# Local attention: masks and turned keys ahead of the output product, statistics at the unit's end

## What is computed

```python
h = shift_token(x)                     # half the features from the row before
q, k, v = split(h @ wqkv)              # 8 heads of 64
q, k = l2norm(q) * qs, l2norm(k) * ks  # norm clipped from below at 1e-12
q, k = rotary_xpos(q, k)
# windows of 128 queries look at the window before and their own:
sim = where(mask, -max, (8 * q) @ k.T)
x = x + (softmax(sim) @ v) @ wo
```

## Time and profile before

| | us |
|---|---|
| median of 3 runs | 3652.75 |
| lowest, highest | 3647.45, 3654.94 |
| profiled execution, its own time | 3663.63 |
| its span, first to last instruction | 3661.8 |
| TensorE busy | 3324.7 (91%) |
| VectorE busy | 1947.9 (53%) |
| ScalarE busy | 1564.8 (43%) |
| GpSimd busy | 569.0 (16%) |
| mean granted TensorE clock | 0.955 |

### The profile page before, as it was taken

How to read it: one execution, slowest core, us unless ns; L and a number is a source line. 1 busy time by engine, 2 the same in 40 slices (tenths; PEclk the granted TensorE clock), 3 DMA queues, 4 the chain that set the end, 5 groups by cost and what they waited for, 6 DMA issues and landing times. The chain is left out here.

```text
span 3661.8 us, 47378 instructions
## 1 busy us (share of the span) xinstructions
PE 3324.7 (91%) x16112; PEld 1955.4 (53%) x16113; DVE 1947.9 (53%) x4733; ACT 1564.8 (43%) x3481; POOL 569.0 (16%) x591
## 2 busy tenths in 40 slices
PE   5999997786999969999998899998899899997998
PEld 3455555553666644444443566665555566665454
DVE  1999996341111125555553677776331677775332
ACT  1766662221222225554554566565221555554211
POOL 0000001442000058000000322221000211111112
PEclk8999998887999979999999999999999999998999
DMA  3000003103111121000000100000000100000000
GB/s 129 1 1 1 1 1 132 36 26 104 44 44 46 44 61 56 4 1 1 1 1 2 62 8 10 9 8 8 21 1 1 37 10 8 10 8 4 12 12 23
DMA packets 72644, 90.25 MB, mean 25 GB/s; under 512 B 10974, under 2 KB 61426, under 8 KB 72178
## 3 DMA queue, kind: packets, MB, share of 16 engines
q1 hardware_dynamic: 65186, 69.28, 5.7%
q0 software_dynamic: 7248, 18.26, 1.6%
HBM read 59.63 MB, written 24.12 MB: 23 GB/s over the span
## 5 line engine op out<-in xcount | busy, mean ns | idle before, releaser
L1619 DVE CUSTOM_DVE_ANT_0 sb_win_masked<-ps_win_pss,sb_win_around 128x384 f32<-128x384 f32 (+1 forms) x512 | 255.6, 538 | 229.9 <-PE ps_win_pss L1726 229.5
L2027 ACT ACTIVATE sb_loc_pr<-ps_loc_psw,sb_loc_nb,sb_loc_sc 128x256 f32<-128x256 f32 x512 | 281.0, 568 | 187.3 <-DVE sb_loc_nb L2154 187.3
L2230 PE MATMUL ps_loc_psa<-sb_stk_w,sb_loc_hT 128*128 128x512 f32 x768 | 350.1, 606 | 5.0 <-DMA sb_stk_wo<-in_loc_wo 3.3
L2517 PE MATMUL ps_mlp_ps<-sb_mlp_hT,sb_stk_w 128*128 128x512 f32 (+1 forms) x768 | 322.6, 613 | 22.3 <-DVE sb_mlp_hid L2470 22.3
L1544 ACT ACTIVATE sb_win_pT<-ps_win_pst 128x512 f32<-128x512 f32 x368 | 199.8, 595 | 207.0 <-PE ps_win_pst L1737 205.2
L2230 PEld LDWEIGHTS ps_loc_psa<-sb_stk_w,sb_loc_hT 128*128 128x128 f32 x768 | 142.0, 192 | 181.4 <-issue 177.8
L2517 PEld LDWEIGHTS ps_mlp_ps<-sb_mlp_hT,sb_stk_w 128*128 128x128 f32 (+1 forms) x768 | 130.2, 184 | 201.6 <-issue 201.6
L719 PE MATMUL ps_rec_psp<-sb_rec_hT,sb_rec_w 128*128 128x512 f32 x512 | 235.4, 603 | 1.0 <-ACT sb_rec_hT L422 1.0
L2470 DVE SCALAR_TENSOR_TENSOR sb_mlp_hid<-ps_mlp_ps,sb_stk_col,sb_mlp_gl 128x512 f32<-128x512 f32 x96 | 71.7, 749 | 303.3 <-ACT sb_mlp_gl L2439 303.3
L2439 ACT ACTIVATE sb_mlp_gl<-ps_mlp_ps,sb_stk_col 128x512 f32<-128x512 f32 x96 | 65.9, 687 | 381.8 <-PE ps_mlp_ps L2517 381.5
L1726 PE MATMUL ps_win_pss<-sb_win_kT,sb_win_q 32*128 32x384 f32 (+1 forms) x1024 | 224.0, 520 | 4.7 <-DVE sb_win_top L1619 3.0
(11 more groups left out here) (316 smaller groups left out, 6560.0 us busy)
## 6 DMA issues: line engine op xcount, KB each, us to landing
sb_exp_rows<-sorted_tokens SPq DMA_DIRECT2D x72, 128.0 KB, 2.0
expert_results<-sb_exp_res SPq DMA_DIRECT2D x72, 128.0 KB, 1.7
sb_keep_x<-in_x SPq DMA_DIRECT2D x1, 4096.0 KB, 23.1
sb_moe_w_in<-in_L_ffn_w_in_eDF SPq DMA_DIRECT2D x8, 512.0 KB, 11.3
sb_moe_w_sw<-in_L_ffn_w_swiglu_eDF SPq DMA_DIRECT2D x8, 512.0 KB, 11.5
sb_exp_w_out<-in_L_ffn_w_out_eFD SPq DMA_DIRECT2D x8, 512.0 KB, 7.0
sb_stk_angles<-in_angles SPq DMA_DIRECT2D x32, 128.0 KB, 3.7
out_y<-sb_stk_y SPq DMA_DIRECT2D x8, 512.0 KB, 3.0
```

Source lines behind the costliest of these rows:

```text
L1619: i = nc.vector.tensor_tensor_reduce(masked[:, pair % 2, j, 0:keys], pss[:, (n + j) % PLAIN, 0:keys], around[:, first:first + keys], 1.0, ...
L2027: e = nc.scalar.activation(pr[:, hf, h], psw[:, hf, h // 2, h % 2 * 256:h % 2 * 256 + 256], ACT.Exp, scale=sc8[:, b, hh:hh + 1], bias=nb[: ...
L2230: t = nc.tensor.matmul(psa[:, c], hT[:, b, k, 1 - k:P + 1 - k], w[:, k, c * 512:(c + 1) * 512], start=(k == 0), stop=(k == KD - 1))
L2517: i = nc.tensor.matmul(ps[at:at + M, q % 2, i2], w1[:, k, i2 * HID + f * P:i2 * HID + f * P + M], hT[:, b, k], start=(k == 0), stop=(k == ...
```

## The change

Five edits, all in `local_attention`. On TensorE, masks(i+1) and turn_keys(i+1) are issued between turn_queries(i+1) and output(i); masks(0) stands ahead of the loop. On VectorE, copy_keys(i+1) moves ahead of add_output(i), and statistics(i+4) to the end of the unit. On ScalarE, copy_input(i+2) goes ahead of deviation(i+4). The lower bound of the squared norms becomes a scalar_tensor_tensor with the same tile as both inputs, max(max(ss, 1e-24), ss), which gives the same value.

```diff
@@ scalar
+                    if i + 2 < TILES:
+                        copy_input(i + 2)
                     if L == 0 and i + 4 < TILES:
                         deviation(i + 4)
-                    if i + 2 < TILES:
-                        copy_input(i + 2)
@@ vector
-                    nc.vector.tensor_scalar(ss[:, b], ss[:, b], 1e-24, None, ALU.max).then_inc(s_ssm, 1)
+                    nc.vector.scalar_tensor_tensor(out=ss[:, b], in0=ss[:, b], scalar=1e-24, in1=ss[:, b], op0=ALU.max,
+                                                   op1=ALU.max).then_inc(s_ssm, 1)
@@
-                    if L == 0 and i + 4 < TILES:
-                        statistics(i + 4)
                     scale_output(i)
                     if i + 1 < TILES:
                         scale_keys(i + 1)
+                        copy_keys(i + 1)
                     add_output(i)
-                    if i + 1 < TILES:
-                        copy_keys(i + 1)
+                    if L == 0 and i + 4 < TILES:
+                        statistics(i + 4)
@@ tensor
+                masks(0)
                 for i in range(TILES):
-                    masks(i)
                     scores(i)
@@
                     if i + 1 < TILES:
                         turn_queries(i + 1)
+                        masks(i + 1)
+                        turn_keys(i + 1)
                     output(i)
-                    if i + 1 < TILES:
-                        turn_keys(i + 1)
```

## The result

The changed kernel takes 3625.61 us (median of 4 runs, 3624.12 to 3626.12), against 3653.85 us for the kernel before in the same comparison (4 runs, 3647.45 to 3658.14). That is 28.2 us less, a ratio of 0.9923 with a 95% interval of 0.9906 to 0.9941 (by these bounds 21.6 to 34.3 us). The forecast was 3627.5.

What follows compares the result with a forecast made beforehand. TensorE bounds the kernel, so only its waiting can be won: 28 units at 0.62 us (17.4) plus 34 at 0.23 (7.8) make 25.2 us off the 3652.75 median, 3627.5 us; range 3617 to 3641.

Steps and rivals of the forecast that it cites:

- Statistics, 0.39 us in 28 units: VectorE, pass 0: statistics moved to the unit's end let the output product start 0.39 us earlier in 28 units.
- unit 28: Pass 0 unit with the 0.70 us bound but no statistics; its output scaling starts 2.08 us after the value products start.
- The norm bound, nothing: VectorE's norm bound as scalar_tensor_tensor: taken as zero gain, even if it still takes 0.70 us.
- Masks and keys ahead: TensorE, before the output product: hides masks in the wait; scores 0.23 us earlier in pass 1, 0.62 with statistics moved.
- V+3.43: Turned keys' forecast start on TensorE, 3.43 us after V, the start of the value products (L2301).
- the step to the scores' shape: TensorE, from transposes to the scores' 64-row shape: price taken as 0.13 us, bounds zero and 0.26.
- V+6.04: Next scores' forecast start on TensorE, 6.04 us after the value products start, against 6.27 before in pass 1.
- (a): GpSimd's second product (L1916) holds up VectorE's L2136 in pass 0: 0.11 us in 28 units, 3630.6 us; chance 9%.
- (b): TensorE's reordering yields nothing, steps between masks, transposes and scores costing 0.23 us a unit more: 3641.8 us; chance 5%.
- (c): Statistics end last before VectorE's maxima, giving back 0.44 us in 28 units: 3639.8 us; chance 3%.
- (d): Denser TensorE work lowers the granted clock in both passes: 0.96 would give 3667 us, slower; chance 3%.

Runs made afterwards that it cites:

- the kernel with early reciprocal and other bank: Changed kernel plus input turned ahead, sums' reciprocal before rotated-key addition, turned sums written to the bank ScalarE empties: 3586.64 us against 3632.87 before, ratio 0.987.

## Why the prediction was right

**What bounds.** TensorE's waiting was all there was to win, and that is what went: TensorE's busy time by the page changed by 3 us, and the clock in the two stretches stayed at 1.00.

**Statistics, 0.39 us in 28 units.** Measured alone: units from 16.31 to 15.92. The reading of unit 28, which has the long bound but no statistics, was enough. What the prediction put less exactly is that the 0.41 us "are the statistics'": they belong to bound and statistics together, since a short bound brought units to 15.92 us as well.

**The norm bound, nothing.** Measured alone 0.9998. The rule from the Trainium skill (SBUF — State Buffer, Who interferes with whom) said that the new form, with its two SBUF inputs, would be held up too. The trace agrees: 0.70 us beside GpSimd's product, 0.19 us for the reduction, which the same section names as never contending. Two inputs are not the whole of it, since the old form with one was held for the same 0.70 us.

**Masks and keys ahead.** The chain on VectorE gave the keys' start at V+3.43 to the hundredth. The term that was mis-sized comes behind it. I took 1.83 us for the output product and 0.13 for the step to the scores' shape, and so V+6.04; the rows of after have 0.49 for the keys, 1.73 for the output product and 0.32 from the turned input to the scores, V+5.97. The 1.83 us were read from a unit in which the output product itself had waited. In the kernel with the masks alone ahead it does not wait, and there it takes 1.73 us to the start of the keys, and the keys 0.43. Now it is the keys that have waited (0.49), and the sum of the two is 2.22 instead of 2.26. The step of shape costs some 0.10 (0.32 less 0.22). Both together are 0.07 us in 62 units, 4 us: by units the change is worth 30 us (15.62 us a unit, where about 15.70 were forecast), and the forecast was 25.2. The measured 28.2 us, with its interval of 21.6 to 34.3, cannot tell the two apart. That the forecast time came within 2 us is thus partly luck.

**The range.** By its own terms, 8 us for the step and 4 for the median, it would be 3615.5 to 3639.5, not 3617 to 3641. The result lies in both.

**Rivals.** (a) L2137 begins beside L1916 and takes 0.68 us, no hold-up; it is GpSimd that is held when it starts second (L1924, 0.93 us instead of 0.46). (b) The reordering did not come out dearer: the steps cost less than taken, not more. (c) The maxima had 0.32 us to spare, 0.36 were worked out. (d) The clock stayed at 1.00 in both stretches.

## What to carry to other kernels

When an in-order engine waits for a short chain on another, list the work that is ready at that moment, put it there, and then follow each result it produces to its reader's queue: the masks and turned keys gained 0.31 us a unit with the keys' copy moved along, and lost 0.75 us (15.92 to 16.67, pass 1) with the copy left behind. A unit of the same loop that lacks one step is a free experiment; it priced the statistics and the bound before anything was built. And where two releasers end within 0.1 us of each other, the one that the trace names may be the wrong one, and only removing both shows their worth.

## What the runs showed of the hardware

A small VectorE instruction can take four times its own time beside GpSimd. The bound, 16 elements wide, takes 0.18 us with GpSimd idle and 0.70 us beside its product in two forms, of which one reads a single SBUF tile; as a reduction it takes 0.19 us at the same place. Where it began 0.16 us behind the start of the product instead of 0.06 (the kernel with early reciprocal and other bank), it took 0.59 us and again ended 0.03 us after the product. It works the other way as well: GpSimd's spread sums took 1.37 us instead of 1.04 when they began 0.16 us after VectorE's addition of two SBUF tiles, and its table 0.93 instead of 0.46 us when it began 0.07 us after VectorE's scaled keys. L2137 was not stretched although it began 0.11 us before the recorded end of L1916, in all 28 units where the two meet; the rows do not say why.
